# A two-layer transformer kernel on one core: all tokens kept transposed, joint keys, three banks for scores, new orders

## The reference

```
# L0 attention: 16 heads of 8, 4 key/value heads
q = x @ Wq + bq ; k = x @ Wk + bk ; v = x @ Wv + bv
attn = softmax(q k^T / sqrt(8)) ; out = (attn v) @ Wo + bo
# L0 ffn: 8 experts share w1, w2, two are picked; the gate weighs one common result
out = combine * (relu(x @ w1) @ w2)
# L1 "attention": a state space layer, DI = 256, 16 states
xs, z = split(x @ W_in) ; xs = silu(conv4(xs)) ; dt = softplus(xs @ W_dt + b_dt) ; Bs = xs @ W_x
h = h * exp(-A * dt) + Bs          # scan over the tokens, one h per state
y = (sum_states(h) + D * xs) * silu(z) ; out = y @ W_out
# L1 ffn, ternary weights
h = silu(x w1) * (x w2) ; h = gelu(h h1) ; h = gelu(h h2) ; out = h w3
```

## Time and profile before

| what | value |
|---|---|
| time, median of 3 runs | 371.86 us (370.92 to 372.0) |
| span of the profiled execution | 370.3 us |
| TensorE busy | 361.6 us |
| VectorE busy | 303.1 us |
| ScalarE busy | 314.4 us |
| GpSimd busy | 238.0 us |
| DMA, all queues | 19.63 MB |

### The profile page before, as it was taken

How to read it: one execution, slowest core, us unless ns; L and a number is a source line. 1 busy time by engine, 2 the same in 40 slices (tenths; PEclk the granted TensorE clock), 3 DMA queues, 4 the chain that set the end, 5 groups by cost and what they waited for, 6 DMA issues and landing times.

```text
span 370.3 us, 5874 instructions
## 1 busy us (share of the span) xinstructions
PE 361.6 (98%) x1810; PEld 185.9 (50%) x1810; DVE 303.1 (82%) x508; ACT 314.4 (85%) x540; POOL 238.0 (64%) x287
## 2 busy tenths in 40 slices
PE   7999999999999999999999999999999999999996
PEld 6757454546454553433324445465445464464546
DVE  4786879978788888579878768989999989998950
ACT  4934878886988887899998899999999999799870
POOL 2156504642527211342989673999999999999990
PEclk9999999999999999999969999999999999999999
DMA  6477282746265220220000000001000000000000
GB/s 217 125 145 147 93 200 35 174 143 120 58 110 123 43 55 2 52 85 0 1 21 3 1 0 2 0 0 48 5 0 21 0 3 28 1 2 1 0 28 28
DMA packets 29902, 19.63 MB, mean 53 GB/s; under 512 B 4496, under 2 KB 28848, under 8 KB 29616
## 3 DMA queue, kind: packets, MB, share of 16 engines
q1 hardware_dynamic: 29872, 19.26, 21.3%
HBM read 13.69 MB, written 5.37 MB: 51 GB/s over the span
## 4 chain that ended last, share of the span: by engine, by line
PE 68%; ACT 8%; DMA 2%; issue 2%; DVE 2%; SPq 0%; POOL 0%; ACTq 0%; DVEq 0%; POOLq 0%
PE bank L908 15%; PE bank L896 13%; PE bank L357 6%; PE bank L980 4%; PE bank L342 4%; ACT da L1088 3%; PE bank L869 3%; PE bank L885 3%; PE bank L886 3%; PE bank L953 3%; PE bank L933 3%; PE bank L388 2%; PE bank L328 2%; PE bank L396 2%; PE bank L970 2%; ACT pt L548 2%
## 5 line engine op out<-in xcount | busy, mean ns | idle before, releaser
L1218 POOL TENSOR_TENSOR acc<-acc,hb 128x512 f32<-128x512 f32 x128 | 158.1, 1273 | 11.6 <-DVE hb L1163 11.2
L1163 DVE TENSOR_TENSOR_SCAN hb<-da,bank 128x512 f32<-128x512 f32 x128 | 145.9, 1200 | 15.1 <-PE bank L869 9.1
L589 DVE TENSOR_REDUCE mx<-bank 128x2 f32<-128x512 f32 x128 | 83.1, 683 | 16.9 <-PE bank L328 14.4
L1088 ACT ACTIVATE da<-dt,nega 128x510 f32<-128x510 f32 x128 | 82.2, 713 | 0.2
L548 ACT ACTIVATE pt<-bank 128x512 f32<-128x512 f32 x128 | 71.2, 596 | 9.8 <-PE bank L342 8.7
L896 PE MATMUL bank<-sil,ld 128*128 128x512 f32 x128 | 59.1, 595 | 0.0
L908 PE MATMUL bank<-gelu,ld 128*128 128x512 f32 x128 | 58.5, 593 | 0.1
L342 PE MATMUL bank<-q_st,k_st 51*128 51x512 bf16 x128 | 42.2, 386 | 1.8 <-ACT pt L548 1.5
L328 PE MATMUL bank<-k_st,q_st 48*128 48x256 bf16 x240 | 38.9, 273 | 0.1
L896 PEld LDWEIGHTS bank<-sil,ld 128*128 128x128 f32 x128 | 24.3, 192 | 26.3 <-issue 25.7
L908 PEld LDWEIGHTS bank<-gelu,ld 128*128 128x128 f32 x128 | 23.8, 190 | 25.6 <-issue 24.7
(11 more groups left out here) (148 smaller groups left out, 534.0 us busy)
## 6 DMA issues: line engine op xcount, KB each, us to landing
q_st<-q_scr SPq DMA_DIRECT2D x8, 384.0 KB, 4.9
q_st<-q_scr SPq DMA_DIRECT2D x15, 192.0 KB, 3.8
ld<-in_pack SPq DMA_DIRECT2D x2, 1024.0 KB, 6.3
q_scr<-qk_parts SPq DMA_DIRECT2D x8, 192.0 KB, 2.1
k_st<-k_scr SPq DMA_DIRECT2D x15, 96.0 KB, 4.5
q_scr<-qk_parts SPq DMA_DIRECT2D x8, 128.0 KB, 2.1
out<-x SPq DMA_DIRECT2D x8, 128.0 KB, 1.9
ld<-in_pack SPq DMA_DIRECT2D x1, 968.0 KB, 5.4
```

What stands on the lines that cost most here:

```text
L589: eng.tensor_reduce(mx[:, 2 * pair:2 * pair + 2, q], s_bank[n % 2][:, :].rearrange("p (h k) -> p h k", h=2), AX.X, ALU.max).then_inc(mx_ok, 1)
L1088: act(da(n)[:, :, 1:T], dt[:, g % 2, c, :].rearrange("p (b n) -> p b n", b=GB)[:, :, 1:T], ACT.Exp, scale=nega[:, c, s:s + 1]).then_inc(da ...
L1163: eng.tensor_tensor_scan(hb[:, s % NPAIR, c, :], da(n).rearrange("p b n -> p (b n)"), b_bank(g, s)[:, :], 0.0, ALU.mult, ALU.add).then_inc ...
L1218: TT(acc[:, g % 2, c, :], acc[:, g % 2, c, :], hb[:, s % NPAIR, c, :], ALU.add).then_inc(add_ok, 1)
```

## The change

- **Tokens transposed.** `xnT` of all eight batches is kept, in the buffer that layer 1 uses later; `xn` has two buffers. `xn_out` waits for no earlier batch any more.
- **Keys.** `project` now gives the queries alone. `project_keys` gives the keys of batch 0, of batches 1 to 3 and of batches 4 to 7 jointly: one product of 32 columns per batch, each in a column tile of its own of one bank. `k_out`, `split_k` and `put_keys` work on such a group at once; `q_out` and `split_q` on 256 columns.
- **Banks.** Query-major scores have three banks (0, 1 and 5). `heads` of batches 0 to 5 goes to bank 6 with the ffn. Bank 7 is halved: one half for transposes, queries and the last keys, the other for values, maxima, `back` and `proj_out`. Tables (`X_AFTER`, `Q_AFTER`, ...) name the evacuation that each of these waits for, also of the other half.
- **Values.** Four value buffers; each is cleared in a step of its own (`clear_values`), three of them later.
- **Loads.** `head` is loaded ahead of the second part of x, which has six tiles instead of four; the ffn weights come last. Semaphores of the stacked data are one per parity.
- **Orders.** All five are new; the number of `warm` pairs stays 44.

```diff
@@ names and buffers
+KEYS = ((0,), (1, 2, 3), (4, 5, 6, 7))
+X_AFTER = "- v0 x1 x2 q1 q2 v1 x6"
+Q_AFTER = "x0 x3 x4 k2 m1 v2 v4 m4"
+V_AFTER = "q0 m0 q4 m2 m3 q7 m5 m6"
+H_AFTER = "f2 h0 f3 f5 f6 f7 p5 p6"
...
-    xnT = [sb(f"xnT_{p}", [P, T]) for p in range(2)]
-    xn = sb("xn", [P, TPB, P])
+    xnT = [t["xnT1"][:, b * T:(b + 1) * T] for b in range(NB)]
+    xn = [sb(f"xn_{p}", [P, TPB, P]) for p in range(2)]
...
-    s_bank, st_bank = banks[0:2], banks[2:4]
+    s_bank, st_bank = (banks[0], banks[1], banks[5]), banks[2:4]
-    bA, bB, bC = banks[5:8]
+    bB, bX = banks[6], banks[7]
+    half0, half1 = bX[:, 0:T], bX[:, T:2 * T]
-    X_PARTS = ((0, TPB), (TPB, 3 * TPB), (3 * TPB, NT))
+    X_PARTS = ((0, TPB), (TPB, 4 * TPB), (4 * TPB, NT))
...
+    def score_free(eng, b, n):
+        if b < LAST:
+            reached(eng, mx_ok, b, NH, n - 2)
...
+    def emptied(eng, before, n):
+        name = before.split()[n]
+        if name == "-":
+            return
+        for signal, per in EMPTIED[name[0]]:
+            eng.wait_ge(signal, per * (int(name[1:]) + 1))
...
         def project(b):
             reached(eng, xnT_ok, b, 1, 1)
-            mm(bA[:, 0:T], wq[:, :], xnT[b % 2][:, :], start=True, stop=True)
+            emptied(eng, Q_AFTER, b)
+            mm(half0, wq[:, :], xnT[b], start=True, stop=True).then_inc(q_ps, 1)
...
-            mm(bA[:, T:2 * T], wk4[:, :], xnT[b % 2][:, :],
-               start=True, stop=True).then_inc(qk_ps, 1)
+        def project_keys(j):
+            reached(eng, xnT_ok, KEYS[j][-1], 1, 1)
...
+            for i, b in enumerate(KEYS[j]):
+                last = mm(key_bank(j)[32 * i:32 * i + 32, :], wk4[:, 0:NKV * HD], xnT[b], start=True, stop=True)
+            last.then_inc(k_ps, 1)
```

More of the change, by code:

```diff
@@ L72 @@
 ORDERS = dict(
[L73 to L85, removed]
-        ffn_out A S proj_out pv max_rows S A S A ffn_in A S A S pv A S v_gate A S A S pv A S A S ffn_in heads A S A
-        S pv S A x_transposes A S A S back ffn_out A S A S x_in proj_out x_in ffn max_rows 2*A pv A pv 2*A x_in ffn
-        x_in A wx A ffn 2*step_in ffn b A x_transposes pv A x_in b x_in A 2*second heads b A x_in A second x_in A b
-        second wx pv A b step_in back A pv A b step_in A b A proj_out 2*A b A 2*pv 2*b 2*second b second b second
-        heads b third back third proj_out b 2*third 2*b 3*third x_transposes third 2*x_in 2*ffn x_in 2*b x_in 2*ffn
-        out wx b 2*second b second b 2*second b second out b step_in b 2*second 2*b 3*out third b out x_transposes b
-        third x_in step_in 2*b 2*third b third b 2*third b x_in third x_in 2*ffn b x_in wx b 2*ffn step_in b out b
-        2*second b second b second b 2*second b second b second 2*out b out b 2*out third b third step_in b third b
-        third b third b third b 2*third b ffn b ffn out b ffn b ffn out b 2*out second b 2*second b second b second
-        b second b 2*second b 2*out b 2*third b 2*third b 4*third 6*out""",
@@ L119 @@
-    gpsimd="""ones G qk_split G biased 6*G qk_split maxima_split 6*G biased 2*G qk_split maxima_split 6*G maxima_split
-        qk_split 3*G biased 7*G maxima_split qk_split 8*G maxima_split qk_split 7*G maxima_split G qk_split G
-        constants 7*G shifted maxima_split 8*G maxima_split split 2*start 3*add start 9*add split 9*add start 7*add
-        shifted 4*add 2*y start 9*add split 23*add start 2*y 2*add start 2*add split add start 27*add 2*y 32*add 2*y""",
+    sync="""x_in head x_in constants0 x_in ffn_weights 3*put 3*put_keys fetch put_keys put 2*put_keys put stack put
+        fetch put rows put 2*rows put fetch 2*put_keys stack put put_keys 3*rows put loads 3*put fetch stack loads put
+        loads 3*rows put fetch stack rows loads rows put rows put fetch stack rows put 2*rows 2*put stack fetch put
+        rows 2*put 2*rows fetch stack 6*rows stack 2*b_rows 2*out b_rows 2*out b_rows 4*out landed""",
@@ L123 @@
+    gpsimd="""3*biased ones G split_k split_q 7*G split_q maxima_split 8*G split_k maxima_split 2*split_q 6*G
+        maxima_split 3*G split_q 3*G maxima_split 9*G split_q G maxima_split 2*G split_q 6*G maxima_split 10*G shifted
+        maxima_split 4*G constants 4*G maxima_split split 2*start 14*add start 5*add split 8*add shifted start 5*add
+        2*y 6*add split 15*add start 11*add y start y 11*add split 2*add start 8*add start 12*add y add y 30*add 2*y""",
 )
@@ L302, in ffn_weights @@
             eng.dma_start(w12[:, :], a["w12"]).then_inc(ld_ffn, 16)
-        return dict(x_in=x_in, head=head, constants0=constants0, ffn_weights=ffn_weights, put=put, fetch=fetch, rows=rows,
+        return dict(x_in=x_in, head=head, constants0=constants0, ffn_weights=ffn_weights, put=put, put_keys=put_keys, fetch=fetch, rows=rows,
                     stack=stack, loads=loads)
@@ L1179, in clear @@
                 settled(eng, done["st_ps"], (NB - 1) * NH)
-                settled(eng, done["stk_ok"], 32 * NB)
+                for p in range(2):
+                    settled(eng, done["stk_ok"][p], 16 * NB)
                 settled(eng, done["y_ok"], NB)
```

348 lines of the change are left out of this document (205 added, 143 removed).

## The result

The changed kernel takes 399.67 us, the median of four runs (394.06 to 400.78), the kernel before beside it 371.49: slower by 28 us, where the forecast was 1.7 us faster and the range ended at 374.0. The two slowest of the four had the lowest mean clock (0.961 and 0.962, the profiled one among them) and are left out of the ratio of 1.0672 (95% interval 1.0602 to 1.0741), which comes to 25 us. The profiled execution has a span of 398.6 us against 370.3.

The account below looks back on a forecast made before the run. TensorE's work was taken as the main bound, with ScalarE at 140 to 191 us and GpSimd nearly late at the end. 1.0 - 2.9 + 0.4 + 0.3 - 2.0 + 1.55 = -1.65 us: 371.86 to 370.2, range 366.5 to 374.0.

Parts of the forecast that it names:

- What bounds the kernel: Whole kernel before: TensorE's work, 341 us; losses at the start and where ScalarE bounds, 140 to 191 us.
- The start, +1.0: Up to the first `A`: maxima 1.2 us later, first `A` at 36.0 against 35.02; bounds -1.0 and +3.
- the second rival: Start: late fetched rows of batch 1 delay the first maxima and eat the gain; 371.9 us, chance 0.20.
- Work up to the hand-over, -2.9: First `A` to last `dt`, TensorE full: joint keys save 1.9 us, other moved work the rest; lower bound 1.4.
- what comes back, +0.4: Same stretch: VectorE and the waits on bank 7 take back 0.4 us, from 0 to 4.
- The slow rival: Layer 0's full batches: bank 7 becomes the bound, one uncovered hand-over per batch; 374.4 us, chance 0.22.
- The hand-over, -2.0 +0.3: Behind the last `E`: one `pv` left at full clock saves 2.0 us; `step_in` between two `A` stalls 0.3.
- GpSimd at the end, +1.55: Layer 1: GpSimd's adds start at 230.9 and end at 363.4 with 0.3 us of gaps; TensorE's product waits, +1.55 us.
- A low clock elsewhere: Sign of being wrong: a low TensorE clock elsewhere, where 1.00 was expected throughout the hand-over.

Follow-up runs that it names:

- the doubled product: The kernel before with the product of the queries made twice in each batch; 375.27 us.
- the repaired kernel: Changed kernel with a second query-parts buffer, SyncE's loads and writes reordered, layer 1 after its first group in the old order, GpSimd's key-tile memsets first; 372.65 us.
- the second buffer alone: Changed kernel with a second buffer for the three parts of a batch's queries, so `q_out` waits for the writes of batch b-2, not b-1; 390.75 us.

## Why the prediction was wrong

**What bounds the kernel** held in the main: with the doubled product, TensorE's work shows nearly in full in the kernel before. But a VectorE maximum shows by half, so VectorE isn't free there.

**The start, +1.0.** Measured +7.2, of which 3.1 are the low clock of the traced execution. The sum for the maxima itself was right: in the repaired kernel the 16th ends at 31.20, where 31.1 was said. The cast held by GpSimd's memset, for which the sum has no term, made it 0.8 us later (32.01). The bound of +3 and the second rival named the other mechanism, the fetched rows of batch 1 in front of `max_rows`: the scores waited 1.0 us for them in the repaired kernel and 1.8 with the second buffer alone. What was never priced is that `q_out` of batch 2 waits (4.13 us) until the last write of batch 1 has landed, behind the first `stack`, and that the transposes wait behind it; by the runs with and without it that is 0.4 us at a full clock, and in the traced execution the low clock follows it. In the repaired kernel +2.1 remain.

**Work up to the hand-over, -2.9, and what comes back, +0.4.** The joint keys cost what was assumed. TensorE's timeline shows the two groups, three and four products side by side, in the length of little more than one (the columns as in the earlier trace rows):

```profile
19.09 0.63 PE L522 MATMUL bank<-xnT,head 128*32 128x256 f32 x6
...
46.07 0.64 PE L522 MATMUL bank<-xnT,head 128*32 128x256 f32 x8
```

From the first `A` to `step_in` the repaired kernel needs 0.5 us less instead of 2.9, so 2.4 came back, inside the bounds of 0 to 4. By its trace 1.25 of it is my repair, the rest isn't settled (neither TensorE nor VectorE alone). So even with every loss repaired the forecast gain of 1.65 us didn't come: the repaired kernel is 1.3 us slower than the kernel before. In the changed kernel itself the stretch took 15 us more. **This is the step that failed**: the edits of SyncE's order were read for the waits of SyncE and for the receivers of the rows, but no transfer was given a landing time behind the megabyte ahead of it, and `q_out`'s wait for landed writes, which the kernel before has as well, was taken as met. So the term for late transfers stood at nothing between the first `A` and the hand-over, and it measured about 15 us with the clock behind it. Before, batch 4's last write (67.16) is issued 11.6 us ahead of the `qk_out` of batch 5 (78.73); in the new order 0.7 us ahead of where `q_out` is ready.

**Bank 7.** The slow rival named the shared bank and said 374.4. The chain through bank 7 did carry the stall to TensorE, but it wasn't its cause: a second buffer elsewhere removed it. The sign of being wrong that the prediction named, idle time of TensorE ahead of transposes (2.10 us at 30.50), came true for this other reason.

**The hand-over, -2.0 +0.3.** The mechanism came, its worth to the kernel isn't shown. ScalarE's last `E` and TensorE behind it, in the changed kernel, which answer to the earlier trace rows:

```profile
179.15 0.69 ACT L1138 ACTIVATE dt<-bank,ld 128x512 f32<-128x512 f32 x1 [0.41 <-PE bank L1031]
...
209.99 0.59 ACT L616 ACTIVATE pt<-bank 128x512 f32<-128x512 f32 x1
```
```profile
210.92 1.06 PE L420 MATMUL bank<-pt,v_sb 128*32 128x512 f32 x8
211.92 0.39 PE L947 MATMUL bank<-b_parts,sel 96*128 96x512 bf16 x1
```

`dt` to `E` takes 30.84 us against 30.88, as said. One `pv` is left, the clock is 1.00, as said. From the last `dt` to the work behind the `pv` it is 32.77 us against 34.35, 1.6 less and not 2.0: the `pv` started 0.4 us late behind a `b` and a `proj_out`. `second` started 2.2 us behind the end of the last `E`, not 1.2: it waited for a `gelu` that stands behind a table load (1.28 us at 210.60), which the sum didn't have. By the first `third` only 0.6 of the 1.6 us are left, less than the kernel before differs from trace to trace there (44.45 to 45.50).

**GpSimd at the end, +1.55.** The first sum of group 1 comes 15.27 us behind the first `x_in` of group 2 (252.82 - 237.55), where 14.8 was said. Then it failed: I allowed 0.3 us of gaps. From 253 us on GpSimd waits for scans as in the first row below, in the kernel before (from 230 us) as in the second:

```profile
POOL acc L1297 <- DVE hb L1241: 15.5, 7, 10.3
```
```profile
POOL acc L1218 <- DVE hb L1163: 1.2, 3, 0.5
```

Without the 10.3 us ahead of the first sum that is 5.2 us. The sum assumed that scans are ready whenever GpSimd is, and they weren't. The orders of the five engines together make them late (above); which step does isn't shown. TensorE waits 0.43 us for the last `y` and not 2, as it was late too.

**The clock.** "A low clock elsewhere" was named as a sign of being wrong; it stood at four places, each behind a wait of TensorE: 2.1 us at 30.50, 6.2 at 73.97, 3.1 at 101.0 and 1.9 at 348.95.

## To carry to other kernels

When an order of DMA issues changes, list each transfer with its size and whoever waits for its landing, a buffer's next writer included, and give a small one the time of what is ahead of it in the queue: a 64 KB write behind 0.86 MB of copies and 0.97 MB of load took 7.3 us, and rows of 8 KB behind such a load alone 4.5, where others took 1.8 to 2.1. Where an order is static on all engines, a wait moves to whatever is issued behind it, so compare the distance between an event and its consumer before and after, not the counts of work. And undo each cheap-looking resource once: the third bank, costed at half a microsecond, was worth 14 with the orders made for it.

## What was not expected of the hardware

- A VectorE cast of 128x256 took 2.00 us beside a GpSimd memset and 0.29 without it; begun late in the memset it took 0.64, and both ended with it.
- Runs of three of the kernels with several stalls spread by 7 to 11 us, in step with the mean granted clock (384.88 us at 0.996, 396.05 at 0.965 of one kernel); two others with stalls spread by 2.3 and 5.3, and the repaired kernel's ten runs by 1.4. A stall costs its length and then some: 6.2 us of waiting were part of a loss of 10, and the same start took 42.24 us at a clock of 0.66 behind its stall and 39.17 at 1.00.
